# TensorE walks image pairs innermost, in the image and in the bank

## What is computed

```python
def _conv(x, w, b):
    y = jax.lax.conv_general_dilated(x, w, window_strides=(2, 2), padding='VALID', dimension_numbers=('NCHW', 'OIHW', 'NCHW'))
    return y + b[None, :, None, None]
xp = jnp.pad(x, ((0, 0), (0, 0), (1, 1), (1, 1)))
xp = xp.at[:, :, DST_R, DST_C].set(xp[:, :, SRC_R, SRC_C])
up = _conv(xp, w_up * jnp.asarray(_UP), b_up)
left = _conv(xp, w_left * jnp.asarray(_LEFT), b_left)
right = _conv(xp, w_right * jnp.asarray(_RIGHT), b_right)
out = out.at[:, :, 0::2, 0::2].set(up)
out = out.at[:, :, 1::2, 0::2].set(left)
out = out.at[:, :, 1::2, 1::2].set(right)
return out * jnp.asarray(OUT_MASK)
...
x = x + _L0_conv_ref(_gn(x), ...)
```

## Time and profile before

| | before |
|---|---|
| median of 3 runs | 799.68 us |
| profiled execution, whole time | 800.35 us |
| its span, first to last instruction | 798.6 us |
| TensorE matmul busy | 707.6 us (89%) |
| TensorE weight loads busy | 638.7 us (80%) |
| VectorE busy | 720.5 us (90%) |
| ScalarE busy | 579.3 us (73%) |
| GpSimd busy | 397.6 us (50%) |
| moved by DMA over the span | 337 GB/s |

### The profile page before, as it was taken

The page is one execution under the profiler, slowest core; times in us unless marked ns, Lnnn a source line. Parts: engine busy times, 40 slices in busy tenths (PEclk is TensorE's granted clock), DMA queues, the critical chain, the costliest instruction groups (busy, mean ns, idle before and its releaser), DMA issues.

```text
span 798.6 us, 36563 instructions
## 1 busy us (share of the span) xinstructions
PE 707.6 (89%) x15762; PEld 638.7 (80%) x15762; DVE 720.5 (90%) x2113; ACT 579.3 (73%) x1258; POOL 397.6 (50%) x795
## 2 busy tenths in 40 slices
PE   0999999999999999999999999999999999999984
PEld 0888887888888888888788888888888888878873
DVE  4899999999999999999999999999999999999950
ACT  2587787787787777778778778777777877877872
POOL 1064464465455456446446545545545644644663
PEclk9999999999999999999999999999999999999997
DMA  9999999999999999999999999999999999997465
GB/s 263 321 364 366 363 354 353 360 350 358 362 350 354 356 356 354 350 361 354 354 362 349 356 363 348 356 361 349 357 354 358 353 353 362 350 355 266 146 223 187
DMA packets 265022, 269.68 MB, mean 338 GB/s; under 512 B 2640, under 2 KB 264784, under 8 KB 264976
## 3 DMA queue, kind: packets, MB, share of 16 engines
q1 hardware_dynamic: 264976, 269.23, 102.1%
HBM read 135.01 MB, written 134.22 MB: 337 GB/s over the span
## 4 chain that ended last, share of the span: by engine, by line
ACT 63%; DVE 22%; issue 10%; PE 2%; DMA 2%; SPq 0%; DVEq 0%; ACTq 0%; POOL 0%; POOLq 0%
ACT tn L321 32%; ACT res L350 30%; DVE stats L222 10%; DVE tn L285 6%; PE bank L447 2%; DVE mate L230 2%; DMA xs<-in_L_conv_w_right 2%; DVE m L235 1%; DVE msum L236 1%; DVE var L243 1%; DVE gap L238 1%; DVE gap L234 1%; ACT xs L363 0%; ACTq L341 0%; SPq L177 0%
## 5 line engine op out<-in xcount | busy, mean ns | idle before, releaser
L447 PE MATMUL bank<-tn,wts 64*64 64x192 f32 (+6 forms) x15600 | 691.3, 323 | 3.9 <-issue 3.9
L447 PEld LDWEIGHTS bank<-tn,wts 64*64 64x64 f32 x15600 | 619.4, 137 | 36.3 <-issue 4.0
L405 POOL TENSOR_TENSOR xs<-res,xs 128x192 f32<-128x192 f32 (+6 forms) x780 | 394.8, 542 | 395.5 <-ACT res L350 395.2
L222 DVE BATCH_NORM_STATS2 stats<-xs 128x6 f32<-128x512 f32 x512 | 341.7, 691 | 8.7 <-DMA xs<-in_x 8.7
L350 ACT ACTIVATE res<-bank,bias 64x512 f32<-64x512 f32 (+6 forms) x650 | 304.1, 468 | 20.3 <-PE bank L447 10.6
L321 ACT ACTIVATE tn<-xs,nmr,rstd 128x256 f32<-128x256 f32 x511 | 258.9, 591 | 4.5 <-DVE nmr L263 2.9
L268 DVE TENSOR_SCALAR tn<-xs,rstd,nmr 128x256 f32<-128x256 f32 x513 | 221.0, 501 | 2.3
L315 ACT ACTIVATE std<-var 128x16 f32<-128x16 f32 x64 | 13.9, 217 | 185.0 <-DVE var L243 185.0
L285 DVE COPY tn<-tn 128x128 f32<-128x128 f32 (+2 forms) x320 | 56.6, 253 | 35.5 <-ACT tn L321 35.4
L459 PEld LDWEIGHTS bank<-blank 128*128 128x128 f16 x130 | 12.5, 96 | 95.0 <-issue 90.2
L459 PE MATMUL bank<-blank 128*128 128x2 f16 x130 | 22.9, 176 | 59.4 <-DVE tn L285 58.5
(11 more groups left out here) (18 smaller groups left out, 33.5 us busy)
## 6 DMA issues: line engine op xcount, KB each, us to landing
xs<-in_x SPq DMA_DIRECT2D x63, 2048.0 KB, 14.6
out<-xs SPq DMA_DIRECT2D x63, 2048.0 KB, 9.0
xs<-in_x SPq DMA_DIRECT2D x4, 512.0 KB, 6.0
out<-xs SPq DMA_DIRECT2D x2, 1024.0 KB, 4.9
xs<-in_L_conv_w_up SPq DMA_DIRECT2D x1, 256.0 KB, 8.3
xs<-in_L_conv_w_left SPq DMA_DIRECT2D x1, 256.0 KB, 9.2
xs<-in_L_conv_w_right SPq DMA_DIRECT2D x1, 256.0 KB, 12.1
bias<-in_L_conv_b_up SPq DMA_DIRECT2D x2, 0.2 KB, 6.9
```

The lines of the kernel that those rows point to most:

```text
L222: last = nc.vector.bn_stats(stats[:, k % 2, 2 * u:2 * u + 2].rearrange("p g a -> p (g a)"), both)
L405: last = nc.gpsimd.tensor_tensor(onto, view(res, at, [(rows * w, pairs), (w, rows), (1, w)]), onto, ALU.add)
L447: last = nc.tensor.matmul(psum[bank + j][to:to + C, at:at + cols], wts[first:first + C, NT * rect[0] + n, :], taps(b, rect, tap, g0, pairs ...
```

## The change

Only the order in which a matmul walks its columns changes. The reads from `tn` now go over rows, then pixels of a row, then pairs, so that neighbouring columns are T_PAIR elements (1224 bytes) apart. The writes go the same way: a new helper, `bank_cells`, walks the bank with the pair innermost, so that neighbouring columns land rows x w cells apart (18, 12, 12, 12 and 8 cells in banks 0 and 1; 12, 6, 8, 7, 4, 6 and 4 in banks 2 and 3). Every value ends in the cell in which it stood before. The number of matmuls, their sizes, weights, waits and order stay, and so do the layouts that all other engines read and write.

```diff
@@ -433,7 +433,11 @@
                 t, r0, c0, rows, dr, dc, w = rect
                 r, c = 2 * r0 + tap[0], 2 * c0 + tap[1]
                 return view(tn[b], g0 * T_PAIR + t_at(r, c),
-                            [(T_PAIR, pairs), (2 * TP * dr + 2 * dc, rows), (2, w)], first, C)
+                            [(2 * TP * dr + 2 * dc, rows), (2, w), (T_PAIR, pairs)], first, C)
+
+            def bank_cells(j, at, rect, pairs, to):
+                t, r0, c0, rows, dr, dc, w = rect
+                return view(psum[j], at, [(w, rows), (1, w), (rows * w, pairs)], to, C)
 
             def bank_taps(b, bank, j, g0, pairs):
 
@@ -445,7 +449,7 @@
                         for first in (0, C):
                             to = C - first if CROSSED[j] else first
                             last = nc.tensor.matmul(
-                                psum[bank + j][to:to + C, at:at + cols],
+                                bank_cells(bank + j, at, rect, pairs, to),
                                 wts[first:first + C, NT * rect[0] + n, :],
                                 taps(b, rect, tap, g0, pairs, first), start=(q == 0 and n == 0),
                                 stop=(n == NT - 1), skip_group_check=True)
```

## The result

The changed kernel takes 1198.52 us (median of four runs, 1197.09 to 1199.93) against 799.62 us for the kernel before (now four runs of it too): a ratio of 1.499, 95% interval 1.497 to 1.502. The forecast was 1146 us, between 1069 and 1301. The profiled execution took 1197.09 us, with a span of 1195.3 us.

A forecast was written before the change was run, and what follows sets the result against it. The chain over ScalarE and VectorE bound the kernel; TensorE would now set the pace. 27.3 us start + 63 chunks x 17.30 = 1089.9, + 17.9 + 1.0 + 8.4 = 1144.5 us span, 1146.3 with 1.75 around it; stated 1146, range 1069 to 1301.

The forecast's parts named there:

- The bound: Chain over VectorE and ScalarE sets 11.80 us a chunk; TensorE needs 10.84 us and has 0.96 us to spare.
- point of decision: Column price, 1.21 ns, at which TensorE's chunk reaches 11.80 us; below it the time does not change.
- Lines and not runs: Matmul reads cost 1.80 ns per 16-byte line of `tn`; the rival, 0.90 ns per run of columns, had chance 0.09.
- A lone column costs as much as two: In matmul reads, a 16-byte line serving one column costs as much as a line serving two.
- The price, 1.80 ns a column: Each column of the changed matmuls reads its own line at 1.80 ns, where it cost about 1.03 in runs of 6.
- runs of 2: Old 64-column matmuls with two neighbouring pixels a row: 91 ns for 48 lines, giving the upper price 1.90.
- main case: Matmuls at 1.67 to 1.90 ns a column: TensorE's chunk 16.1 to 18.2 us, time 1069 to 1206 us; chance 0.74.
- fixed part: 163 ns of each matmul's duration, independent of its lines, taken as latency overlapping the next matmul.
- The writes: Bank writes with gaps add nothing if overlapping reads; up to 2.06 ns a column, 1301 us, had chance 0.07.
- Balance and overhead: Gate, start, drain and uneven array shares in TensorE's two stretches: 0.60 us a chunk, 0.50 to 0.85.
- Start: First chunk's lower clock level costs nothing extra, since its 1.69 ns a column lies under 1.80.
- End: Last chunk outside the loop 17.9 us plus 1.0 us issue wait, then 8.4 us after the last matmul.

The follow-up runs named there:

- only_w2: Kernel before, with the new column order only for bank 3's two rectangles with w = 2: 801.47 us, ratio 0.9999.
- evac_first_held: Kernel before, with banks 0 and 1 evacuated ahead of `root(k)` and GpSimd's first add held until the later chunk's variance: 756.64 us, ratio 0.945.
- steps of 4, 12 and 16 bytes: Kernel before, reading a row's pixels 4, 12 or 16 bytes apart instead of 8 (wrong pixels, same work): 801.72, 954.12 and 1150.75 us.
- pitches 320 and 352: Changed kernel with T_PAIR, the pitch from pair to pair, at 320 or 352 elements instead of 306: 1094.24 and 1094.12 us.
- 4-byte step: Kernel before, reading a row's pixels 4 bytes apart instead of 8 (wrong pixels, same work): 801.72 us.
- 16-byte step: Kernel before, reading a row's pixels 16 bytes apart instead of 8 (wrong pixels, same work): 1150.75 us.
- write_gap: Kernel before, reads in the old order, each column written 64 bytes from the last and GpSimd's add reading the bank in that order: 848.28 us, ratio 1.061.

## Why the prediction was right, point by point

**The bound.** Right. TensorE had 0.96 us a chunk to spare; `only_w2` used up half of it at no cost, and `evac_first_held` shortened the chain until VectorE's own work bound it, with TensorE 0.1 us below. That the point of decision is 1.21 ns a column follows from this; no run lay close to it.

**Lines and not runs.** The rows of before could not tell them apart, and I gave the run a chance of 0.09. The steps of 4, 12 and 16 bytes, with runs as before, decided for lines.

**A lone column costs as much as two.** Right, and it is the step on which the result hangs. The Trainium skill (SBUF — State Buffer, Door 1: The DMA port swizzle, its note on cachelines) asks for two hits on a 16-byte line; the 1.69 ns of a lone column at the pitches 320 and 352 agree with it, being twice the 0.82 ns of a column in the 4-byte step within 0.05 ns. At the other pitches a lone column costs more than two.

**The price, 1.80 ns a column.** This term was mis-sized: 1.89. It holds for lines that are neighbours (the 16-byte step: 1.78 ns a column and 1150.75 us, where the sum said 1146), but the change puts them 76.5 lines apart. The upper bound of 1.90, taken from the runs of 2, held it only just, and by luck: with 308 in place of 306 elements the main case would have missed, at 2.00 ns and 1281 us against its 1206 us, and only the part of the range kept for the writes would have covered it. That the distance between lines might matter was in no term of the sum. The fixed part was mis-sized as well, 180 ns for 163, so that 288 columns last 725 ns and not 681; it overlaps the next matmul and adds nothing to a chunk.

**The writes.** Free, as the sum took them; the bound of 2.06 ns was not needed. It also rests on a slip: 201 ns for 192 columns are 1.05 ns a column and not 1.03, and the durations less 163 ns give 1.05 to 1.42 where the text has 1.03 to 1.36. The bound would be 2.09 ns and the top of the range about 1321 us; nothing of the result hangs on it. The Trainium skill (PSUM — Partial Sum Buffer, Specifications) says that any access with gaps slows matmuls significantly; the trace of these fp32 matmuls, which take no column faster than about 1 ns, disagrees: 315 ns for 128 columns with gaps of 64 bytes and 315 without.

**Balance and overhead.** 9280 x 1.893 = 17.57 us, so 0.52 us a chunk are left of 18.09, where 0.60 were taken. **Start.** The first chunk's matmuls lasted 731 and 542 ns where they had lasted 684 and 522, about as in the rest of the run (725 and 543), so the start cost nothing extra, as said. That they ran at the lower level is taken over from the durations of before: the clock line shows 1.00 there in both traces. **End.** The last chunk took 19.3 us (1167.59 to 1186.9) against 18.9, and 8.4 us followed, as said.

**The sum.** 63 chunks x (18.10 - 17.30) = 50.4 us, and 0.4 at the end: these 50.8 us lie between the 1146.3 us of the sum and the 1197.1 us of the profiled execution. The price of a line makes up all of it: 0.87 us a chunk, of which the balance gives 0.08 back.

## What to carry to other kernels

Count the 16-byte lines that the moving operand of an fp32 matmul touches, and price a line as its columns but never less than two of them (the distance between lines added up to 0.31 ns to that here); an order of the loops in which neighbouring columns share lines is worth a factor of 1.7 in TensorE's time here (10.84 against 18.09 us a chunk). Ask the chain of waits first how much of that time is spare: here 9% was, and a matmul could be made slower or faster within it without a trace in the result. When an engine's step is moved forward, look at what it releases: the adds that followed gave back nearly all of the gain until they were held in place.

## What the runs showed of the hardware that I had not expected

- The price of a far line depends on the pitch: 2.00, 1.89, 1.83, 1.70 and 1.69 ns at 77, 76.5, 78, 80 and 88 lines, and 1.78 ns for lines that are neighbours. Two elements more of padding cost 83 us, fourteen more gained 104 us.
- Writing a bank with gaps of 64 bytes costs a matmul nothing (281 and 281 ns for 112 columns), at a pace of about 1 ns a column and slower.
- GpSimd's adds slow small VectorE operations that run beside them (198 to 498 ns for a copy of 32 elements), and its reads at 64 bytes make it worse (VectorE's normalising 501 to 630 ns), while BATCH_NORM_STATS2 stays (691 and 686 ns).
- TensorE's granted clock over 400 to 600 us was 0.94 in the 4-byte step, which waits 1.5 us a chunk for the wrap copies, 0.96 in `write_gap`, which waits 1.4 us, and 1.00 in the kernel before, which waits 0.96 us. No wait of this kind was longer than 2.2 us there. That the waits are the cause was not tried by itself.
